# The diagonal 16x16 blocks of a triangular inverse by forward substitution on VectorE, in place of three levels of products on TensorE

## What is computed

```
K, V, Q = x @ thK.T, x @ thV.T, x @ thQ.T
for each token:                       # W, b carried along, for each of 2 sequences
    g = 2/512 * (W @ k + b - v)
    W = W - 0.01 * outer(g, k);  b = b - 0.01 * g
    out = W @ q + b
x = layernorm(x + out)
logits = x @ rW.T + bias;  a = sqrt(softplus(logits));  top 2 of 8
x = layernorm(x + shared(x) + sum over the two of a_e * expert_e(x))
```

## Time and profile before

| | us |
|---|---|
| median of 3 runs | 2592.84 (2590.72 to 2592.88) |
| profiled execution | 2602.65 |
| its span, first to last instruction | 2600.8 |
| TensorE busy in the span | 2416.2 (93%) |
| VectorE busy | 1522.9 (59%) |
| ScalarE (ACT) busy | 939.6 (36%) |
| GpSimd (POOL) busy | 1178.8 (45%) |
| granted TensorE clock, mean | 0.968 |

### The profile page before, as it was taken

How to read it: one execution, slowest core, us unless ns; L and a number is a source line. 1 busy time by engine, 2 the same in 40 slices (tenths; PEclk the granted TensorE clock), 3 DMA queues, 4 the chain that set the end, 5 groups by cost and what they waited for, 6 DMA issues and landing times.

```text
span 2600.8 us, 42889 instructions
## 1 busy us (share of the span) xinstructions
PE 2416.2 (93%) x14690; PEld 2133.4 (82%) x14690; DVE 1522.9 (59%) x2788; ACT 939.6 (36%) x1981; POOL 1178.8 (45%) x1117
## 2 busy tenths in 40 slices
PE   6999999999999999999999999658999988898875
PEld 5888888888888888888888888547889877787764
DVE  4555555555556555555556655445444667767778
ACT  3323233332333232333323332254445544444441
POOL 1234433433442455445444554523432456546667
PEclk8999999999999999999999999788999999999997
DMA  3011101111110111111111110376674666767675
GB/s 138 33 40 44 48 33 43 48 41 37 41 53 33 41 46 45 33 45 45 41 37 41 54 34 29 86 199 194 128 139 152 209 220 223 222 193 225 216 236 185
DMA packets 134144, 256.97 MB, mean 99 GB/s; under 512 B 38256, under 2 KB 38512, under 8 KB 133296
## 3 DMA queue, kind: packets, MB, share of 16 engines
q1 hardware_dynamic: 96640, 181.49, 21.4%
q0 software_dynamic: 26256, 72.71, 10.6%
q10 hardware_dynamic: 11040, 0.04, 0.2%
HBM read 161.49 MB, written 92.68 MB: 98 GB/s over the span
## 4 chain that ended last, share of the span: by engine, by line
PE 69%; DMA 8%; POOL 8%; issue 8%; DVE 4%; ACT 2%; DVEq 0%; SPq 0%; another core or an unknown queue 0%; POOLq 0%; ACTq 0%
PE banks L104 19%; PE banks L98 16%; PE banks L100 15%; PE banks L99 15%; DMA b_XN<-x1d,IDX 3%; POOL RG L1574 3%; DMA RG<-ys,POS 2%; POOL b_Y L1464 1%; POOL b_XN L1562 1%; PE banks L594 1%; PE banks L391 1%; PE banks L470 1%; POOL b_sd L1464 1%; DMA b_Y<-x1d 1%; DMA ids<-idt,POS 1%
## 5 line engine op out<-in xcount | busy, mean ns | idle before, releaser
L98 PE MATMUL banks<-W 128*128 128x512 f32 (+1 forms) x2040 | 754.4, 370 | 10.1 <-DVE W L914 10.1
L100 PE MATMUL banks<-W 128*128 128x512 f32 (+1 forms) x2040 | 717.2, 352 | 0.0
L99 PE MATMUL banks<-W 128*128 128x512 f32 (+1 forms) x2040 | 717.0, 351 | 0.0
L100 PEld LDWEIGHTS banks<-W 128*128 128x128 f32 x2040 | 387.2, 190 | 52.9
L98 PEld LDWEIGHTS banks<-W 128*128 128x128 f32 x2040 | 389.0, 191 | 49.1 <-POOL W L1464 8.6
L99 PEld LDWEIGHTS banks<-W 128*128 128x128 f32 x2040 | 389.4, 191 | 38.6
L1464 POOL TENSOR_TENSOR W<-S,W 128x512 fp32r<-128x512 f32 x248 | 314.0, 1286 | 226.9 <-DVE S L914 206.5
L104 PE MATMUL banks<-W,b_XH 128*128 (+1 forms) x1704 | 328.1, 290 | 0.0
L1488 POOL TENSOR_SCALAR sd<-mv 128x1 f32<-128x1 f32 x64 | 14.4, 225 | 658.0 <-DVE mv L1002 658.0
L658 ACT ACTIVATE W<-banks 128x512 fp32r<-128x512 f32 x320 | 187.2, 595 | 341.7 <-DVE banks L914 219.7
L104 PE MATMUL banks<-W,b_XL 128*128 (+1 forms) x852 | 262.3, 308 | 37.4 <-DVE b_XL L914 34.9
(11 more groups left out here) (124 smaller groups left out, 4103.2 us busy)
## 6 DMA issues: line engine op xcount, KB each, us to landing
ys<-b_Y SPq DMA_DIRECT2D x149, 256.0 KB
XT<-in_xT SPq DMA_DIRECT2D x32, 512.0 KB
X<-in_x SPq DMA_DIRECT2D x32, 512.0 KB, 4.0
x1d<-X SPq DMA_DIRECT2D x64, 256.0 KB, 2.0
x1td<-XTo SPq DMA_DIRECT2D x64, 256.0 KB, 2.1
b_XN<-x1td SPq DMA_DIRECT2D x64, 256.0 KB
b_Y<-x1d SPq DMA_DIRECT2D x64, 256.0 KB
out<-b_Y SPq DMA_DIRECT2D x64, 256.0 KB
```

Of the source, the lines that this page charges most:

```text
L98: e.matmul(o, ll, rh, start=start, stop=False, skip_group_check=True)
L99: e.matmul(o, lh, rl, start=False, stop=False, skip_group_check=True)
L100: return e.matmul(o, lh, rh, start=False, stop=stop, skip_group_check=True)
```

## The change

- Constants: `LEVELS` is 16, 32, 64, so `NL` is 3. The six bf16 level masks (`levb`) go; a level's mask is now three times 8 numbers a partition, in the small table, broadcast over 16 columns each. `cst` has three masks instead of four, the third for the diagonal 16x16 blocks; the loaded table of masks has 2 x 128 columns instead of 8 x 128.
- `scores`: the two passes into `MM` and the addition of the identity go. New are a pass into `T1` with the block mask and a sum over the 8 blocks (`Gd`, 2 x 16 columns), which leaves for each partition its row of its own block.
- SP writes `Gd` to memory (`blocks_out`) and reads it back in eight transfers (`blocks_in`), each of which gives all 16 partitions of a block all of that block's numbers (`Lb`, 16 x 2 x 16).
- `subst`: each partition then solves for one column of its block's inverse. `x` starts as a column of the identity, and for j = 0 to 14 and both b one instruction adds `Lb[j] * x[j]` to the rest of `x`. These are 15 pairs of instructions on 15 down to 1 columns, with a scalar read from memory; each waits for all before it but the last.
- `inv_m`: VectorE spreads `x` into the 128x128 form `MM[1]` (block diagonal), TensorE transposes it for both b, ACT copies the result into `MM[0]`.
- Order: the substitution lies between the four `s_part(t, 0, ec)` on VectorE; `inv_m(n)` behind `s_part(t, 1, 0)` on VectorE, and between the two bias products on TensorE. T0 of step n comes at the end of step t, in front of `p_part(n, 0)`; N0, T1, N1, T2, N2 come in the first half of the next step.
- Before the loop, step 0's inverse is made by the same parts in a row.

```diff
-LEVELS = [2, 4, 8, 16, 32, 64]
+BS = 16
+NBL = P // BS
+LEVELS = [16, 32, 64]
...
@@ first_memory
-        k.levb = sb("levb", [NL, P], BF16)
+        k.Gd, k.Lb, k.x = sb("Gd", [NB, BS]), sb("Lb", [BS, NB, BS]), sb("x", [NB, BS])
@@ tensor_program
+    def inv_m(t):
+        o = bank(w, ("MM", t), k.s_M0, t + 1)
+        w.wait_ge(k.s_M, NL * t + 1)
+        for b in range(NB):
+            z = e.transpose(o[:, b * P:(b + 1) * P], k.MM[:, 1, b, :], ident)
+        z.then_inc(k.s_MM, 1)
...
     for t in range(NT):
         n, more = t + 1, t + 1 < NT
         p_part(t, 0)
-        inv_t(t, 4)
+        inv_n(t, 0)
         p_part(t, 1)
-        inv_n(t, 4)
+        inv_t(t, 1)
         if more:
             k_proj(n, 0)
-        inv_t(t, 5)
+        inv_n(t, 1)
         if more:
             q_proj(n, 0, 0)
             k_turn(n, 0)
+        inv_t(t, 2)
+        if more:
             k_proj(n, 1)
-        inv_n(t, 5)
+        inv_n(t, 2)
...
         if more:
             v_proj(n, 0)
-            inv_t(n, 0)
             v_proj(n, 1)
-            inv_n(n, 0)
             s_part(t, 0, 0)
             s_part(t, 0, 1)
-            inv_t(n, 1)
...
             s_part(t, 1, 3)
             b_part(t, 0)
-            inv_n(n, 3)
+            inv_m(n)
             b_part(t, 1)
         logits(t, 1)
+        if more:
+            inv_t(n, 0)
@@ scalar_program
+    def inv_m(t):
+        w.wait_ge(k.s_MM, t + 1)
+        w.wait_ge(k.s_T, NL * t)
+        copy(k.MM[:, 0, :, :].rearrange("p b n -> p (b n)"), at["MM", t][:, 0:256]).then_inc(k.s_M0, 1)
...
             s_part(t, 1, 3)
+            inv_m(n)
             if t + 2 < NT:
                 split_xt(t + 2)
@@ vector_program, scores
-        w.wait_ge(k.s_MThi, t)
-        w.wait_ge(k.s_MTlo, t)
+        stt(k.T1[:], g, 1.0, mBD.unsqueeze(1).to_broadcast(bc), ALU.add, ALU.mult).then_inc(k.s_sc, 1)
         stt(k.LT[:], g, 1.0, mLT.unsqueeze(1).to_broadcast(bc), ALU.add, ALU.mult).then_inc(k.s_sc, 1)
-        for j in range(2):
-            stt(k.MM[:, j, :, :], g, 1.0, m1[:, j, :].unsqueeze(1).to_broadcast(bc), ALU.add, ALU.mult).then_inc(k.s_sc, 1)
+        w.wait_ge(k.s_sc, 4 * t + 1)
+        w.wait_ge(k.d_gd, 16 * t)
+        e.tensor_reduce(k.Gd[:], k.T1[:].rearrange("p b (k j) -> p b j k", k=NBL), AX.X, ALU.add).then_inc(k.s_sc, 1)
         stt(kq, kq, -1.0, mAT.unsqueeze(1).to_broadcast(bc), ALU.add, ALU.mult).then_inc(k.s_sc, 1)
-        w.wait_ge(k.s_sc, 4 * t + 3)
-        mmv = k.MM[:].rearrange("p k b n -> p (k b) n")
-        tt(mmv, mmv, k.ident[:].unsqueeze(1).to_broadcast([P, 2 * NB, P]), ALU.add).then_inc(k.s_M, 1)
...
+    def subst(t):
+        n0 = (2 * BS - 1) * t
+        w.wait_ge(k.s_M, NL * (t - 1) + 1)
+        w.wait_ge(k.d_tab, 80)
+        e.tensor_copy(k.x[:], k.smallc[:, 16:32].unsqueeze(1).to_broadcast([P, NB, BS])).then_inc(k.s_sub, 1)
+        yield
+        w.wait_ge(k.d_lb, 16 * NBL * (t + 1))
+        for j in range(BS - 1):
+            for b in range(NB):
+                w.wait_ge(k.s_sub, n0 + max(1, 2 * j + b))
+                rest = k.x[:, b, j + 1:BS]
+                stt(rest, k.Lb[:, j, b, j + 1:BS], k.x[:, b, j:j + 1], rest, ALU.mult, ALU.add).then_inc(k.s_sub, 1)
+            yield
+
+    def inv_m(t):
+        w.wait_ge(k.s_sub, (2 * BS - 1) * (t + 1))
+        w.wait_ge(k.s_MThi, t)
+        w.wait_ge(k.s_MTlo, t)
+        tt(in_cells(k.MM[:, 1, :, :]), k.x[:].unsqueeze(2).to_broadcast(cells), by_cell(blocks), ALU.mult).then_inc(k.s_M, 1)
...
@@ vector_program, before the loop
-    inv_t(0, 0)
-    inv_n(0, 0)
...
+    split_state(0)
+    split_state(1)
+    for _ in subst(0):
+        pass
+    inv_m(0)
+    inv_t(0, 0)
@@ vector_program, in the loop
+            blocks_of_n = subst(n)
+            for ec in range(KC):
+                s_part(t, 0, ec)
+                tick()
+                for _ in range(4):
+                    next(blocks_of_n, None)
...
+            for ec in range(KC):
+                s_part(t, 1, ec)
+                tick()
+                if ec == 0:
+                    for _ in blocks_of_n:
+                        pass
+                    inv_m(n)
...
@@ sync_program
+    def blocks_out(t):
+        w.wait_ge(k.s_sc, 4 * t + 3)
+        w.wait_ge(k.d_lb, 16 * NBL * (t - 1))
+        e.dma_start(k.gd[t % 2].rearrange("k (i n) -> (k i) n", i=BS), k.Gd[:].rearrange("p b j -> p (b j)")).then_inc(k.d_gd, 16)
+
+    def blocks_in(t):
+        w.wait_ge(k.d_gd, 16 * (t + 1))
+        w.wait_ge(k.s_sub, (2 * BS - 1) * t)
+        for x in range(NBL):
+            e.dma_start(k.Lb[x * BS:(x + 1) * BS].rearrange("p i b j -> p (i b j)"),
+                        k.gd[t % 2, x:x + 1, :].broadcast_to([BS, BS * NB * BS])).then_inc(k.d_lb, 16)
...
+        if t + 1 < NT:
+            blocks_out(t + 1)
         norm(t, 0)
+        if t + 1 < NT:
+            blocks_in(t + 1)
         norm(t, 1)
```

More of the change, by code:

```diff
@@ L133, in program @@
     k.zd = nc.dram_tensor("zd", (NTL, P, D), F32, kind="Internal").ap()
+    k.gd = nc.dram_tensor("gd", (2, NBL, BS * NB * BS), F32, kind="Internal").ap()
     k.ids = [nc.dram_tensor(f"ids{g['x']}", (g["slots"] * P, 1), I32, kind="Internal").ap() for g in k.groups]
@@ L516, in tensor_program @@
     v_proj(0, 0)
+    v_proj(0, 1)
+    inv_m(0)
     inv_t(0, 0)
-    v_proj(0, 1)
-    inv_n(0, 0)
-    for n in range(1, 4):
-        inv_t(0, n)
-        inv_n(0, n)
     for t in range(NT):
@@ L563, in tensor_program @@
         if more:
[L564 to L568, removed]
+            for ec in range(3):
+                s_part(t, 1, ec)
         turn_x1(t, 1)
         if more:
-            inv_t(n, 3)
             s_part(t, 1, 3)
             b_part(t, 0)
-            inv_n(n, 3)
+            inv_m(n)
             b_part(t, 1)
         logits(t, 1)
+        if more:
+            inv_t(n, 0)
         for g in k.groups[:-1]:
@@ L751, in scalar_program @@
     w.wait_ge(k.d_lev, 16)
-    copy(k.onesr[:], k.RG[:, NL * P:NL * P + P]).then_inc(k.s_ones, 1)
+    copy(k.onesr[:], k.RG[:, 0:P]).then_inc(k.s_ones, 1)
     k_proj(0, 0)
@@ L909, in vector_program, with in_cells, by_cell @@
     at = k.banks.at
-    mLT, mAT, m1 = k.cst[:, 0, :], k.cst[:, 1, :], k.cst[:, 2:4, :]
+    mLT, mAT, mBD = (k.cst[:, j, :] for j in range(NCST))
+    levels, blocks = k.smallc[:, 40:64].rearrange("p (n k) -> p n k", n=NL), k.smallc[:, 128:136]
+    cells = [P, NB, NBL, BS]
+    def in_cells(x):
+        return x.rearrange("p b (k j) -> p b k j", k=NBL)
+    def by_cell(x):
+        return x.unsqueeze(1).unsqueeze(3).to_broadcast(cells)
     bc = [P, NB, P]
@@ L1224, in vector_program @@
     scores(0)
-    inv_t(0, 0)
[L1226 to L1231, removed]
-    split_state(1)
-    inv_t(0, 3)
-    inv_n(0, 3)
+    split_state(0)
+    split_state(1)
+    for _ in subst(0):
+        pass
+    inv_m(0)
+    inv_t(0, 0)
     routes = []
@@ L1299, in vector_program @@
         tick()
-        if more:
-            tick()
-            inv_t(n, 0)
-            tick()
         norm(t, 1)
@@ L1659, in sync_program @@
     e.dma_start(k.idt[:], a["ids"]).then_inc(k.d_tab, 16)
-    e.dma_start(k.RG[:, 0:NL * P + 2 * P], a["lev"]).then_inc(k.d_lev, 16)
+    e.dma_start(k.RG[:, 0:2 * P], a["ones"]).then_inc(k.d_lev, 16)
     w.wait_ge(k.s_thlo, KC)
@@ L1670, in sync_program @@
         load_xt(1)
+    blocks_out(0)
+    blocks_in(0)
     if NT > 2:
@@ L1764, in constants @@
     r, c = i[:, None], i[None, :]
-    up, low = (r < c), (r > c)
-    def lev(s, a, b):
-        return (a // s == b // s + 1) & ((a // s) % 2 == 1)
-    m = [up * LRC, (r <= c) * -1.0, -LRC * lev(1, r, c), -LRC * lev(1, c, r)]
-    levels = np.concatenate([lev(s, r, c) * 1.0 for s in LEVELS] + [np.ones((P, P)), up * 1.0], 1)
-    return np.ascontiguousarray(np.stack(m, 1).astype(np.float32)), levels.astype(np.float32)
+    up, k = r < c, np.arange(NBL)[None]
+    blocks = r // BS == k
+    levels = [(r // x == k * BS // x + 1) & ((r // x) % 2 == 1) for x in LEVELS]
+    masks = np.stack([up * LRC, (r <= c) * -1.0, np.repeat(blocks, BS, 1) * -LRC], 1), np.concatenate([np.ones((P, P)), up * 1.0], 1)
+    return [np.ascontiguousarray(x.astype(np.float32)) for x in (*masks, np.concatenate(levels, 1), blocks)]
 def kernel(**inputs):
@@ L1782 @@
     NT = S // P
-    cst, lev = constants()
+    cst, ones, levels, blocks = constants()
     arrays = {
@@ L1792 @@
         "cst": cst,
-        "lev": lev,
+        "ones": ones,
         "ident": np.eye(P, dtype=np.float32),
@@ L1808 @@
     small[:, E:2 * E] = E - np.arange(E)
+    small[:, 16:32] = np.arange(P)[:, None] % BS == np.arange(BS)[None]
     small[:, 32:40] = 1.0
-    small[:, 64:] = np.arange(80)
+    small[:, 40:64] = levels
+    small[:, 64:128] = np.arange(64)
+    small[:, 128:136] = blocks
     arrays["small"] = small
```

58 lines of the change are left out of this document (13 added, 45 removed).

## The result

The changed kernel takes 2752.76 us (median of 4 runs, 2742.3 to 2761.64), beside 2592.86 for the kernel before on the same chip. The ratio is 1.0608, interval 1.0563 to 1.0653: **6% slower**, where the prediction had it faster, and outside its range. The profiled execution took 2742.3.

A forecast was written before the change was run, and what follows sets the result against it. TensorE's own instruction order was taken as the bound. Windows -63.2, work behind them +28.5, routing +7 and start -2 sum to -29.7 us: 2563 against the median 2592.84, range 2520 to 2612.

The forecast's parts named there:

- TensorE's order: TensorE's work behind the next step's first state product: T and N moved there, +0.89 us in each of 32 steps.
- the window: From a step's scores to the next step's first state product, p_part(n,0): forecast 2.04 us shorter, 31 times, -63.2 in all.
- The price of an instruction: VectorE's substitution: each instruction 0.22 us long, the next starting 0.14 after it, so 0.28 a pair.
- B: Rival: the scalar read from memory costs nothing, 1.35 us a window less, 42 in all, total 2521; chance 0.17.
- D: Rival: no two substitution instructions overlap, +3.75 us a window, +116, total 2679; chance 0.20.
- The 15 pairs of the substitution: On VectorE between the state updates: 4.2 us, within an unbroken string of 8.3 us up to s_part(t,1,2).
- S: Theory formed after the measurement: a VectorE instruction with both inputs in SBUF stands still while GpSimd reads SBUF.
- I cost no fall of the clock.: TensorE would wait 2.6 us a step, in two or three pieces, without its clock falling; costed at nothing.
- Transfers: Gd's write and eight reads back: blocks land at 961 in the middle, hidden by 1.0 us, up to 1.6 late.
- C: Rival: the blocks come late, by 1.6 us in each window, +50, total 2613; chance 0.15, half of it slower.
- Routing steps: Four steps with routing instructions strewn between VectorE's others, for which there is no room left: +7 us.
- Start: Before the loop: smaller mask load, first inverse swaps products for a round trip and bare substitution; -2 us, bounds -6 to +4.

The follow-up runs named there:

- the memset: Changed kernel with GpSimd's low-part subtraction for b = 0 replaced by a memset of the same tile; 2591.09 us in a single run.

## Why the prediction was wrong

- **TensorE's order.** T, N and the transposes behind the window: 28.7 forecast, 28.73 measured in the quickest steps. The order was right. With seven banks it is 29.1.
- **The price of an instruction.** 0.22 long, 0.14 from one to the next, 0.28 a pair, and no full stop between dependent ones: all measured. The Trainium skill's rule that I weighed (page VectorE: DVE Perf Modes, section The DRAIN you can't avoid) was rightly not followed here. I had read it too strictly: the same section says that a next operation that isn't held starts earlier. B and D fall. D's period (53.5, where the quickest steps take 54.20) comes nearest by accident, and its total, 2679, is still 74 short: it spreads over 30 instructions what four of them have.
- **The step that failed** is "The 15 pairs of the substitution ... 15 x 0.28 = 4.2" in "From there VectorE has one unbroken string". The string has four stops of 1.0 to 1.1 us, in which VectorE stands while GpSimd reads. What failed is the assumption that a term worked out from VectorE's own rows holds whatever GpSimd does. From the first update to s_part(t,1,2) it takes 12.6 us (534.59 to 546.61 + 0.60) instead of 8.3, and beside the memset it takes 8.4 (547.82 to 555.64 + 0.60). I looked for the price of an instruction, and not at who works beside it. GpSimd's low parts lay in the same window before (four in a row from 964.13), harmless, since VectorE's updates there have an input in PSUM. The Trainium skill's rule quoted under S was there to read, and the trace of before shows the stop. In its second phase, from 1700 to 2600 us, the same subtraction has one input in PSUM or both in SBUF (tile `b_XL`, ns, min/median/max):

```profile
L914 DVE TENSOR_TENSOR b_XL<-banks,b_XH x149: 676/692/694, 1761.0 to 2486.5; 128x512 fp32r<-128x512 f32 x149
L914 DVE TENSOR_TENSOR b_XL<-b_XN,b_XH x64: 674/683/2477, 1703.3 to 2571.9; 128x512 fp32r<-128x512 f32 x64
```

  With one input in PSUM none is over 694 ns, and 128 of the 149 lie beside GpSimd's work. With both in SBUF the 27 that lie beside none take at most 693, and 18 of the 37 beside GpSimd's work take longer, up to 2477.

  With 12.6 - 8.4 = 4.2 more in the string the window would have been forecast at 25.2 (measured 25.47), and the sum 31 x 4.2 = 130 higher: 2693.
- **"I cost no fall of the clock."** Wrong, and a second term put at nothing: the clock in the loop is 0.93. The waits came out longer (2.36 and 1.08 us), but a wait of 1.27 us is followed by falls too, in about half of the steps with `x` in PSUM. 55.40 in the mean less 54.20 in the quickest steps, times 31, is 37 us.
- **The window without the stops** is 21.3 to 21.5 instead of 21.0, some 10 us in all. The three make 177; the phase came out 169 over its forecast (1728.0 against 1586.3 - 63.2 + 28.5 + 7 = 1558.6). The 8 between them I can't place.
- **Transfers.** The write of `Gd` landed after 1.4 us, the reads after 1.7 to 3.4, and VectorE has no wait for them: right, C falls. The last of the eight issues starts 3.4 us after the first, where I had 2.3 to 2.9 (528.50 and 531.87), but the landing lies inside the bounds. In the window shown the blocks are there at 533.71 and wanted at 535.48: 1.8 us of room where I had said 1.0. With the string moved forward it is not enough.
- **Routing steps.** +7 forecast. With `x` in PSUM the first three such periods are 53.3, 55.75 and 51.1 beside 50.5, 8.6 over; before, they were 51.96, 52.29 and 50.87 beside 50.87, 2.5 over. That is 6 for two of the four steps, some 12 for all.
- **Start.** -2 forecast. Step 1's scores are ready at 85.48 us instead of 84.47: 1 us later, within the bounds.
- **The trade itself.** That taking products off TensorE in exchange for a string on VectorE could pay was right: with the stops out of the way and the string in VectorE's idle gap it gains 2.25%.

## What to carry over

Before moving work to VectorE, list what GpSimd does in that stretch, and count the inputs that the new instructions have in SBUF: with two, each GpSimd instruction that reads SBUF may stop VectorE for its whole length, and one operand in PSUM ends that. When the mean of a group is far above its median, find the long ones and look at what the other engines have at that moment. A wait filled with idle products isn't gone if another engine's string ends when it did: it turns up at the next wait, and the clock may fall there.

## What was not expected of the hardware

- A VectorE instruction of 0.22 us took 1.33 beside a GpSimd subtraction of 1.28, and one of 0.42 took 1.10. Beside a memset none of 391 was held, and with one input in PSUM none of 960.
- An instruction that waits for the last but one of its kind and takes its scalar from memory starts 0.14 us after the one before, 0.08 before that one's end.
- Waits of 1.24 and 1.23 us, in steps of the same form, were followed by a granted clock of 0.63 in one and 1.00 in the other, and with `x` in PSUM and no fill a wait of 1.27 was followed by a fall in some steps and by none in others. What decides it stays open.
